# Two-row-block attention kernel: triangular levels and inverse in compact 32-column blocks, turned by VectorE

## What is computed

```
q, k, v = silu(conv4(h @ wq)), silu(conv4(h @ wk)), silu(conv4(h @ wv))    # per head: 128 channels
g    = -exp(A_log) * softplus(h @ f_a @ f_b + dt_bias);  beta = sigmoid(h @ b_w)
q, k = l2norm(q) / sqrt(128), l2norm(k)
def step(St, (qt, kt, vt, gt, bt)):                # a scan over the tokens
    St = St * exp(gt)[..., None]
    err = kt @ St
    St = St + bt * outer(kt, vt - err)
    ot = qt @ St
o = rmsnorm(o * sigmoid(gate)) * onorm_w;  x = x + o @ wo
```

## Time and profile before

| | us |
|---|---|
| median of 3 runs | 9731.81 |
| the profiled execution, its time | 9727.55 |
| its span, first to last instruction | 9725.8 |
| PE (TensorE matmuls) busy | 9201.2 (95%) |
| PEld (TensorE weight loads) busy | 6238.5 (64%) |
| DVE (VectorE) busy | 6905.9 (71%) |
| ACT (ScalarE) busy | 6786.5 (70%) |
| POOL (GpSimd) busy | 3460.7 (36%) |

### The profile page before, as it was taken

How to read it: one execution, slowest core, us unless ns; L and a number is a source line. 1 busy time by engine, 2 the same in 40 slices (tenths; PEclk the granted TensorE clock), 3 DMA queues, 4 the chain that set the end, 5 groups by cost and what they waited for, 6 DMA issues and landing times. The chain is left out here.

```text
span 9725.8 us, 368049 instructions
## 1 busy us (share of the span) xinstructions
PE 9201.2 (95%) x137172; PEld 6238.5 (64%) x137172; DVE 6905.9 (71%) x12288; ACT 6786.5 (70%) x15797; POOL 3460.7 (36%) x5963
## 2 busy tenths in 40 slices
PE   4799999999999999999999999999999999988888
PEld 2576667677676767676666666676767666663333
DVE  2677778788787877777878787787878787872111
ACT  1677777777777777777777787777777777861121
POOL 0344434444343434443444444443444344430000
PEclk7899999999999999999999999999999999998988
DMA  0211111111111111111111111111111111120000
GB/s 28 53 40 38 38 38 38 39 38 40 37 40 37 39 38 39 38 39 38 38 39 38 39 38 39 37 39 38 38 39 38 39 38 38 39 62 4 9 9 12
DMA packets 514020, 351.68 MB, mean 36 GB/s; under 512 B 63136, under 2 KB 510752, under 8 KB 512816
## 3 DMA queue, kind: packets, MB, share of 16 engines
q1 hardware_dynamic: 511760, 328.31, 13.1%
q0 software_dynamic: 1088, 4.26, 0.1%
HBM read 289.94 MB, written 42.47 MB: 34 GB/s over the span
## 5 line engine op out<-in xcount | busy, mean ns | idle before, releaser
L1186 POOL TENSOR_TENSOR KB<-KB,tot 128x256 f32<-128x256 f32 x1290 | 998.6, 774 | 3755.2 <-PE bank L599 3755.2
L1254 DVE SCALAR_TENSOR_TENSOR acc<-bank,hp,acc 128x510 f32<-128x510 f32 (+2 forms) x2331 | 1718.6, 745 | 76.5 <-ACT hnew L882 12.7
L552 PE MATMUL bank<-hn,w_qkv 128*128 (+1 forms) x3108 | 1521.0, 612 | 2.5 <-issue 2.2
L1312 DVE COPY_PREDICATED BIG<-masks,bank 128x512 f32<-128x512 int32 x1032 | 1040.3, 1008 | 251.2 <-PE bank L599 242.9
L1351 DVE TENSOR_TENSOR invT<-invT,bank 64x128 f32<-64x128 f32 x2576 | 739.6, 287 | 456.7 <-PE bank L650 428.3
L899 ACT ACTIVATE Zm<-bank 64x128 f32<-64x128 f32 x2576 | 704.6, 274 | 429.0 <-PE bank L626 403.9
L1324 DVE TENSOR_TENSOR QKF<-QKF,tot 128x512 f32<-128x512 f32 x1289 | 980.9, 761 | 1.3 <-PE bank L599 1.2
L599 PE MATMUL bank<-QKF,KB 128*64 128x64 f32 x20640 | 887.0, 228 | 0.7 <-issue 0.4
L665 PEld LDWEIGHTS bank<-ident,invT 128*128 128x128 f32 x5152 | 608.1, 141 | 299.6 <-issue 145.5
L665 PE MATMUL bank<-ident,invT 128*128 128x128 f32 x5152 | 791.0, 276 | 7.2 <-DVE invT L1351 3.4
L552 PEld LDWEIGHTS bank<-hn,w_qkv 128*128 128x128 f32 x3108 | 530.9, 190 | 408.9 <-issue 379.5
(11 more groups left out here) (207 smaller groups left out, 20224.8 us busy)
## 6 DMA issues: line engine op xcount, KB each, us to landing
bb<-beta_rows SPq DMA_DIRECT2D x520, 128.0 KB, 4.1
states<-StC SPq DMA_DIRECT2D x288, 128.0 KB, 1.9
w_qkv<-in_L_attn_wk_dram SPq DMA_DIRECT2D x260, 128.0 KB, 2.2
w_qkv<-in_L_attn_wq_dram SPq DMA_DIRECT2D x260, 128.0 KB, 2.2
w_qkv<-in_L_attn_wv_dram SPq DMA_DIRECT2D x260, 128.0 KB, 3.1
StA<-states SPq DMA_DIRECT2D x259, 128.0 KB, 2.1
w_o<-in_L_attn_wo_dram SPq DMA_DIRECT2D x257, 128.0 KB, 2.0
w_fb<-in_L_attn_f_b_dram SPq DMA_DIRECT2D x260, 64.0 KB, 4.0
```

The source lines that it names most:

```text
L552: mm = eng.matmul(rows(BK["proj_" + "qkv"[n_]]), w_qkv[:, n_, k, :], hn_v[:, k, :, cols], start=(k == 0), stop=(k == KD - 1))
L1186: eng.tensor_tensor(e_, e_, t_.to_broadcast([P, C, P // (2 * m), m]), ALU.mult).then_inc(ev[f"kb_mul{s}"], 1)
L1254: eng.scalar_tensor_tensor(dst, rows(bk)[:, :, 0:BLK - sh], hp[par][:, w_:w_ + 1], dst, ALU.mult, ALU.add).then_inc(ev[("tap_" if t_ < 2 e ...
L1312: eng.copy_predicated(dst, mk, ps).then_inc(ev[f"lvl_e{s}"], 1)
```

## The change

The levels 0 to 4 and the inverse up to level 4 live in compact form: for each chain only the four 32 x 32 blocks on the diagonal are kept, as a tile of 128 partitions x 4 chains x 32 columns. Pieces:

- `CMP` (slots 0 for q.k, 1 to 4 for k.k of that level, 5 for the inverse) takes the place of `BIG`, `IE` of `invE`, `ZC` of `Zm` for levels up to 5. Level 0 to 4 and `diag` make 4 products of 32 columns for each chain where there were 2 of 64. Level 5 and its z and y products keep 2 for each chain, of 32 columns where they were 64 wide. The z and y products of levels 1 to 4, which had 4 of 32 columns before, now move 16 columns where they moved 32 (the inverse's even or odd blocks of one 32-column block).
- `turn` and `first_inverse` are gone from TensorE. VectorE turns `CMP`'s inverse slot to `IE` with one `transpose`, which turns each 32 x 32 block by itself (`turn_inverse`, `turn_corner`). Beta is stored negated, so that the signs work out and VectorE copies by mask into the inverse where it subtracted before.
- Levels 5 and 6 need the full matrices: GpSimd spreads `CMP` and `IE` to `QA`, `IN` and `ZT` with copies of one 32-partition quarter each (`spread_scores` 4, `spread_inverse` 4, `spread_corner` 2). ScalarE copies level 4 no more, but copies the results of levels 5 and 6 of the inverse (`take_inverse5`, `take_inverse6`). `grow_keys(6)` moves from ScalarE to GpSimd.
- `QKF`, `vs`, `qsq`, `hp`, `tott` have 4 buffers (2 before), `KB`, `IE`, the upper `tot` 2. The pipeline is deeper: `step(i)` reaches to i+5 on TensorE (i+4 before), the prologue has 6 steps (4 before).
- The new order of every engine, and a new bank table `AT`. TensorE's `read` list grows: before each group it names every reader of that bank. TensorE's loop body holds 32 steps (16 before), with a hint for its back edge; the others' hold 4. `open_out` and `close_out` are gone: the first and last head's products open and close the sum.
- The masks and a 32-column identity are loaded by quarters, 20 transfers where there were 4.

```diff
-            QKF = [sb(mid, f"QKF{i}", [P, 2, C, P]) for i in range(2)]
-            BIG = sb(mid, "BIG", [P, LEVELS + 2, C, P])
-            Zm = [None] + [tile4(f"Zm{s}") for s in range(1, LEVELS)]
-            invT = [tile4(f"invT{i}") for i in range(2)]
+            QKF = [sb(mid, f"QKF{i}", [P, 2, C, P]) for i in range(4)]
+            CMP = [sb(mid, f"CMP{i}", [P, SLOTS, C, QUART]) for i in range(2)]
+            IE = [sb(mid, f"IE{i}", [P, C, QUART]) for i in range(2)]
+            ZC = [None] + [sb(mid, f"ZC{s}", [P, C, QUART]) for s in range(1, LEVELS - 1)]
+            QA = [sb(mid, f"QA{i}", [P, 2, C, P]) for i in range(2)]
+            IN = tile4("IN")
+            ZT = sb(mid, "ZT", [P, C, HALF])
...
+        if s < 5:                                                      # level
+            for ch in range(C):
+                for q4 in range(4):
+                    rw = quarter(q4)
+                    mm = eng.matmul(ps[rw, :, ch, :, :], kb[:, ch, rw],
+                                    QKF[p][:, :, ch, rw].rearrange("p f (n two m) -> p f n two m", two=2, m=m)[:, :, :, 1, :],
+                                    start=True, stop=True)
...
-                    def turn(s, tile, par):
-                        eng.wait_ge(ev[f"inv_m{s}"], done(tile))
-                        for ch in range(C):
-                            mm = eng.transpose(chains(BK[f"t{s}"])[:, ch, :], invT[par][:, ch, :], ident[:, :])
-                        mm.then_inc(ev[f"t_tr{s}"], 1)
...
-                        read(eng, "z_cp3", i + 1)
-                        if on(i):
-                            state(1, i)
+                        read(eng, "diag_cp", i + 2)
+                        read(eng, "lvl_e1", i + 2)
+                        read(eng, "lvl_e2", i + 2)
+                        read(eng, "St_up0", i)
+                        read(eng, "lvl_e3", i + 2)
+                        read(eng, "gate_t", i)
+                        read(eng, "z_cp5", i + 1)
+                        if on(i + 3):
+                            diag(i + 3)
...
+                    with nc.Fori(0, NO, engines=(mybir.EngineType.PE,), hint_back_edge=True) as o:
+                        for k in range(HTOT):
+                            step(o * HTOT + k, k)
...
+                    def spread_scores(j, p):                            # GpSimd
+                        for q4 in range(4):
+                            rw = quarter(q4)
+                            if q4:
+                                eng.wait_ge(ev["sp_q"], 3 * (j + PRE) + q4)
+                            eng.tensor_copy(QA[p % 2][rw, 0, :, rw], CMP[p % 2][rw, 0, :, :]).then_inc(ev["sp_q" if q4 < 3 else "qnat"], 1)
...
+                    def grow_inverse(s, tile, p):                       # VectorE
+                        eng.copy_predicated(pairs(CMP[p % 2][:, INV, :, :], s)[:, :, 1, :], mk,
+                                            area(f"y{s}", C * HB).rearrange("p (cn m) -> p cn m", m=m)).then_inc(ev[f"y_e{s}"], 1)
+                    def turn_inverse(s, j, p):
+                        eng.transpose(IE[p % 2][:, :, :], CMP[p % 2][:, INV, :, :]).then_inc(ev[f"inv{s}"], 1)
```

More of the change, by code:

```diff
@@ L344, in adaln_kernel @@
             AO0, AO1 = 6, 7
[L345 to L350, removed]
@@ new lines, in area, with chains, rows, half @@
+            def area(name, n):
+                b_, lo = AT[name]
+                return bank[b_][:, lo:lo + n]
+            def chains(name):
+                return area(name, C * P).rearrange("p (c n) -> p c n", c=C)
+            def rows(name):
+                return area(name, C * P).rearrange("p (b n) -> p b n", b=B)
+            def half(name):
+                return area(name, B * P).rearrange("p (b n) -> p b n", b=B)
+            def scores(name, n):
+                return area(name, 2 * C * n).rearrange("p (f c n) -> p f c n", f=2, c=C)
@@ new lines, in y_product @@
+                                    mm = eng.matmul(ps[rw, ch, :, :], ZC[s][rw, ch, :], split(c_[rw, INV, ch, :], s)[:, :, 1, :], start=True, stop=True)
+                        elif s == 5:
+                            for ch in range(C):
+                                for h in range(2):
+                                    lo, hi = quarter(2 * h), quarter(2 * h + 1)
+                                    mm = eng.matmul(small("y5", QUART)[lo, ch, :], ZC[5][hi, ch, :], c_[hi, INV, ch, :], start=True, stop=True)
@@ L866, in _ @@
+                        read(eng, "tap2_v", i + 5)
+                        read(eng, "tap2_k", i + 5)
+                        read(eng, "kb_cp", i + 2)
+                        read(eng, "lvl_e0", i + 3)
+                        if on(i + 4):
+                            level(0, i + 4, (k + 4) % 4)
+                    block_now = [None]
                     start_counts(eng, "pe")
                     eng.wait_ge(ready, N_READY)
-                    loop(eng, step, begin_block, lambda o: close_out(), HTOT // 2)
+                    for i in range(-PROLOGUE, 0):
+                        step(i, i % HTOT)
@@ L1462, in _ @@
                     eng.sem_inc(ready, 1)
+                    for i in range(AO0):
+                        eng.memset(bank[i][:, :], 0.0).then_inc(ready, 1)
                     eng.wait_ge(ready, N_READY)
                     eng.sem_inc(ao_out, 1)
-                    loop(eng, step, None, end_block)
+                    loop(eng, step, end_block)
         end_phase()
```

1298 lines of the change are left out of this document (733 added, 565 removed).

## The result

The changed kernel takes 10609.22 us (median of 4 runs, 10538.23 to 10677.13) where the kernel before took 9730.61 beside it: a ratio of 1.0906, 95% interval 1.0817 to 1.0994. The forecast was 9200 us, the range ended at 9660. The profiled execution took 10659.03 us.

A forecast was written before the change was run, and what follows sets the result against it. TensorE's instruction stream was taken as the bound: a step of 32.0 − 3.1 − 1.4 − 0.6 − 0.5 + 3.5 + 0.3 = 30.2, taken as 30.1 us; 9727.55 − 255 × 1.9 − 45 = 9198, forecast 9200 us, range 9000 to 9400.

The forecast's parts named there:

- What bounds the kernel: Whole kernel: TensorE's own instruction stream is the path, its matmuls busy for 95% of the span, other engines 71% or less.
- the step of 32.0 us: TensorE's loop body before the change: one step takes 32.0 us inside a body, read from the sum over channels.
- the jumps: Jumps back between TensorE's loop bodies: 10 us each, 15 before and 7 after the change, −80 us.
- the entry: Before the steps: two more steps of filling +30 us, mask transfers and clearing of buffers +5 us.
- What leaves TensorE, −3.1: Five turns at 0.49 to 0.50 us and the first inverse at 0.58 leave TensorE: −3.1 us a step.
- narrower tiles, −1.4, −0.6, −0.5: Per step: `diag` and levels 0 to 4 −1.4 us, level 5 with z and y −0.6, fewer tile-form changes −0.5.
- The waits, +3.8: TensorE's waits, 64 to 149 a step: +3.5 us behind 14 groups of 32 passes, +0.3 behind level 5's three groups.
- The formula: A 32-pass TensorE group followed by k waiting instructions costs about 0.27 + 0.105(k−1) us.
- The other engines, nothing: VectorE about 22 us a step, ScalarE about 20, GpSimd 17.3, all beside TensorE's 30; nothing charged.
- the slower one: Rival: 128x32 products of `diag` and levels 0 to 4 don't run four at a time; about 9940 us, chance 0.11.
- Waits are hidden: Rival: TensorE's redundant waits cost only 0 to 1.5 us a step; 8280 to 8790 us, chance 0.12.
- another engine's chain on top: Rival: VectorE's transposes or GpSimd's quarter copies are several times dearer, delaying TensorE; 9425 to 9655 us, chance 0.15.

The follow-up runs named there:

- e1_once: Changed kernel with TensorE waiting for each reader of a bank once per tile, 193 of 229 bank waits left out; 9244.7 us.
- e3_long: Changed kernel without the 101 repeated waits behind the other (not narrow) groups, those behind narrow groups kept; 10525 us.
- e2_short: Changed kernel without only the 92 repeated waits behind narrow groups, the other repeats kept; 9369 us.
- e4_before_more: Kernel before, with four waits repeated ahead of each of TensorE's 41 bank waits; 10115 us.
- e11_fill: Changed kernel, all waits kept, plus two more products adding zeros, behind diag and level 2, in 31 of 32 steps; 10338 us.
- e9_two: Changed kernel with at most two bank waits ahead of a group, 67 waiting instructions a step; +26 us against e1_once.
- e8_four: Changed kernel with at most four bank waits ahead of a group, 102 waiting instructions a step; 9597 us.
- e5_spread: e1_once with out_product between level 4 and level 0, residual(0) ahead of z3 and project(2) behind level 1; 9528 us.
- e6_out_only: e1_once with only out_product moved, to between level 4 and level 0; 9226 us.
- e7_nohint: e1_once without the hint for the back edge of TensorE's loop; 9205 us.

## Why the prediction was wrong

- *What bounds the kernel, the step of 32.0 us, the jumps*: held as a reading of before. The term for the jumps was too careful: −113 us, where −80 was said; the entry was right (+37 for +35). All outside the steps came to −88 us for −45, within the 80 us that it allowed itself.
- *What leaves TensorE, −3.1, and narrower tiles, −1.4, −0.6, −0.5*: right in sum. With the 3.8 for waits taken off again the working gives 26.4 us, and the line fitted to `e1_once` gives 26.4 for a step without half clock and silences. Its fastest step takes 26.9; its 41 steps without half clock take 28.0, with 1.7 us of silences in them. 128x32 tiles cost 0.35 to 0.46 a group for the 0.39 taken.
- *The waits, +3.8*: right in size and in place. Between the two fitted lines lie 30.5 − 26.4 = 4.1 us. The steps at full clock say much the same: the changed kernel's are 2.6 us above those of `e1_once` (30.6 against 28.0) and hold 1.6 us less of silences, 4.2 together. `e3_long` and `e2_short` show the place. The formula was too high for the kernel before: 82 more waits cost 1.5 us there.
- *The other engines, nothing*: right in the main; their busy times came within 2 us a step of the estimates. Between 4000 and 5000 us the longest wait of TensorE for another engine is level 0's for ScalarE's copy `ZC`, 12.6 us in 6 times, 0.5 us a step. `e1_once` has it too (10.8 us in 6 times).
- *The step that failed* is one that the prediction did not weigh at all: it took TensorE's clock, 0.99 in the earlier trace rows, as given. Its sum of 30.1 us has no term for the clock, and the steps that do run at full clock take 30.6. The measured mean is 36.0, with the clock at half for 10.6 us of it. That costs 5.2 us a step by the steps' own slope (0.49 × 10.6), 4.6 by the line with silences in it. Without it the profiled time would be 10659 − 255 × 5.2 = 9333 us, or 9486 by the 4.6: 4 or 2% under the kernel before, where the prediction had 5%. The rows to see it were there: the earlier trace rows shows 0.76 where TensorE was busy for only 7.5 of 14 us, and the prediction itself worked out that 14 narrow groups would each take 0.25 us more for waits, which it then charged as time and not as idle. A page of the Trainium skill that was used, "TensorE: Matmul & The Clock Gate", has the rule in the section named above; it would have been a rival, ending on the slow side.
- *A smaller one*: the silences, 1.2 us a step in the changed kernel, which go with the loading of TensorE's own instructions. Before, where narrow groups stood apart, they hardly showed. They were in none of the rivals.
- *The rivals*: the slower one had the right sign by a wrong mechanism (128x32 tiles at 1.2 us a group, measured 0.46 in the rows above). "Waits are hidden" is refuted by `e1_once`; "another engine's chain on top" was seen in the changed kernel only as the 0.5 us above, and came out stronger only when the order was moved.

What is shown: that the repeated waits make the loss and where they stand decides (`e1_once` to `e4_before_more`), that the clock is a cost of its own (`e11_fill`) and goes down further with more waits behind the narrow groups (`e9_two`, `e8_four`), that long runs of narrow groups make the silences (`e5_spread`, `e6_out_only`). Argued only, from fits to the steps, is the split of the changed kernel's 9.6 us over 26.4 into waits 4.1, half clock 4.6 and silences 0.9. The same reading accounts for what holds the versions without repeated waits at 30 us: half clock and silences, 1.5 and 2.7 us in `e1_once`. Open is how to be rid of the silences without a wait in their place.

## What to carry to other kernels

Count the instructions that only wait, and look where they stand: behind a long group they were nearly free here (51 of them cost 0.5 us a step), while the 44 that `e3_long` kept behind narrow groups of 0.35 us or so cost 4.9 us a step, the clock's part included. Don't ask only what an idle of 0.2 us between groups costs, ask what it does to TensorE's clock, if a run of such groups stands ahead of dense work; the granted clock by windows shows it at once. Wait for each reader once per tile: removing 193 repeats of 229 turned a kernel that was 9% slower into one that is 5% faster.

## Unexpected of the hardware

- TensorE went silent for 0.6 to 2.6 us, 1.0 times a step in the changed kernel and 1.5 times in `e1_once`, mostly around the loading of a 16 KB piece of instructions during a run of narrow groups.
- Adding two products of 0.86 us a step made the kernel 2.6% faster (10338 for 10609 us).
- A hint for the back edge took 3 us off a jump (0.9 us over other steps in `e1_once`, 4.1 in `e7_nohint`); but the changed kernel, which has the hint too, still shows 4.6.
- 82 more waits cost 1.5 us a step in the order of before, 95 more cost 5.4 in the new one, the clock's part included.
